# Deformable convolutions on quarters of the matrix array: sums, row spreads and offset convolution in quarter tiles, half-bank sums, row tents' high parts on GpSimd

## What is computed

```python
# x: (4, 64, 24, 24) f32
x = x + _L0_conv_ref(_gn(x), ...)
x = x + _L1_conv_ref(_gn(x), ...)

# one layer, in short
off = conv3x3(x, w_off) + b_off              # 18 offset channels (layer 1: + 9 mask channels)
py = base_y + ky + off_y; px = base_x + kx + off_x
val = corner(y0, x0, wy0 * wx0) + corner(y0, x0 + 1, wy0 * wx1) \
    + corner(y0 + 1, x0, wy1 * wx0) + corner(y0 + 1, x0 + 1, wy1 * wx1)
out = einsum('bckhw,ock->bohw', val * mask, w_def) + b_def
# layer 1 alone: relu(groupnorm over the sample(out))
```

## Time and profile before

| | us |
|---|---|
| median of 3 runs | 170.42 (170.38 to 170.93) |
| the profiled execution | 170.41 |
| its span | 168.6 |
| TensorE busy | 148.6 |
| VectorE busy | 104.9 |
| ScalarE busy | 105.8 |
| GpSimd busy | 68.0 |

### The profile page before, as it was taken

How to read it: one execution, slowest core, us unless ns; L and a number is a source line. 1 busy time by engine, 2 the same in 40 slices (tenths; PEclk the granted TensorE clock), 3 DMA queues, 4 the chain that set the end, 5 groups by cost and what they waited for, 6 DMA issues and landing times.

```text
span 168.6 us, 4694 instructions
## 1 busy us (share of the span) xinstructions
PE 148.6 (88%) x1640; PEld 112.4 (67%) x1640; DVE 104.9 (62%) x248; ACT 105.8 (63%) x243; POOL 68.0 (40%) x131
## 2 busy tenths in 40 slices
PE   7999977999998989997888999998788988979920
PEld 2466634699897766774666876774666867969910
DVE  0526668987675564369986675359975667753133
ACT  3014678889768465379777575379787657864201
POOL 8601355354454434235154434235154425541011
...
GB/s 196 286 251 202 96 34 148 66 2 4 0 6 0 6 2 45 146 60 0 0 4 0 0 8 44 146 61 2 0 6 0 0 10 0 2 70 4 4 6 70
DMA packets 12757, 8.38 MB, mean 50 GB/s; under 512 B 3052, under 2 KB 11820, under 8 KB 12728
## 3 DMA queue, kind: packets, MB, share of 16 engines
...
q10 hardware_dynamic: 288, 0.27, 0.5%
...
## 4 chain that ended last, share of the span: by engine, by line
PE 72%; DVE 12%; issue 9%; ACT 4%; POOL 1%; POOLq 0%; DVEq 0%; ACTq 0%
PE vb L986 18%; PE ob L1006 18%; PE ob L907 11%; PE ring L943 9%; PE ring L951 8%; DVE s L765 5%; PE vb L1081 3%; ACT xa L575 2%; PE ring L895 2%; DVE msk L718 2%; PE ring L926 2%; DVE pos L711 1%; DVE ytent L757 1%; PE ring L885 1%; ACT off L526 1%
## 5 line engine op out<-in xcount | busy, mean ns | idle before, releaser
L487 POOL TENSOR_SCALAR xa<-xa 125x384 f32<-125x384 f32 x108 | 57.5, 538 | 70.1 <-ACT xa L575 69.5
L765 DVE SCALAR_TENSOR_TENSOR s<-xa,ring 125x384 f32<-125x384 f32 x108 | 58.3, 551 | 32.9 <-PE ring L943 28.8
L575 ACT ACTIVATE xa<-ring 125x384 f32<-125x384 f32 x108 | 51.4, 488 | 17.8 <-PE ring L951 17.0
L1006 PE MATMUL ob<-val,w_d 128*64 128x192 f32 x432 | 42.6, 326 | 0.0
L951 PE MATMUL ring<-pos,soon 68*64 68x384 f16 x216 | 37.5, 329 | 3.8 <-DVE s L765 3.1
L943 PE MATMUL ring<-ytent,soon 128*64 128x384 f16 x216 | 37.4, 328 | 3.1 <-DVE ytent L757 1.3
L986 PE MATMUL vb<-s,shifted 125*64 125x216 f32 (+2 forms) x376 | 34.9, 305 | 0.9 <-DVE s L765 0.9
L1006 PEld LDWEIGHTS ob<-val,w_d 128*64 128x64 f32 x432 | 33.7, 136 | 2.5 <-issue 0.4
L986 PEld LDWEIGHTS vb<-s,shifted 125*64 125x64 f32 x376 | 24.5, 136 | 5.0 <-ACT xa L575 1.3
L598 ACT ACTIVATE val<-vb 128x432 f32<-128x432 f32 x33 | 17.5, 530 | 7.4 <-PE vb L986 6.0
L951 PEld LDWEIGHTS ring<-pos,soon 68*64 68x64 f16 x216 | 14.3, 109 | 9.8 <-issue 3.7
...
## 6 DMA issues: line engine op xcount, KB each, us to landing
...
```

The source lines that it names most:

```text
L487: nc.gpsimd.tensor_scalar(v, v, 1.0, 0.0, ALU.min, ALU.max).then_inc(xu_ready, 1)
L575: nc.scalar.activation(xa[:, n % XA_BUFS, :], bank("x", n)[0:SPAN, 0:2 * UPX], ACT.Abs).then_inc(act_took, 1)
L765: nc.vector.scalar_tensor_tensor(out=s[u % 2][:, k // 3:k // 3 + 2 * THIRD, W * k:W * (k + 1)], in0=xa[:, n % XA_BUFS, :].rearrange("q (r ...
L1006: last = mm(sums[64 * i:64 * i + 64, 0:UPX], w_d[l][:, t, 64 * i:64 * i + 64], val[u % 2][:, t // 3:t // 3 + THIRD, W * t:W * (t + 1)], st ...
```

## The change

Seven things change together:

1. The weighted sums use a contraction of 64 lanes (one sample) and 96 pixels, so that a tap is four matmuls on the array's four quarters; their result lies in halves `h` of the unit's rows, `h` = 0 in bank 0 on the samples' own lanes and `h` = 1 in bank 1 on crossed lanes. What reads them does so in three pieces.
2. The offset convolution uses one sample per row half and a quarter of the image per 32 columns: eight matmuls of 144 pixels per tap instead of two of 288. Its result takes two banks of the ring, and ACT reads it in two pieces.
3. The row tents' lanes are rearranged so that a tap's high and low parts lie in one half of the lanes (even taps in lanes 0 to 63, odd taps in 64 to 127). A row spread has a contraction of 64 lanes.
4. Column spreads, row distances and masks have a contraction of at most 60 lanes instead of 68 and 91 (`OFF_LANES`, `MLO`).
5. The high part of the row tents is formed by POOL instead of ACT.
6. The weight blocks lose their zero half; `w_o` is half as large, and two clearing instructions of POOL and a wait of SyncE go.
7. The tables give other orders; a chunk of windows has two parts with due times of their own; the convolutions are one job each; the idle quarters go.

```diff
-OFF_LANES = 68
+OFF_LANES = 60
-MLO = 64
+MLO = 32
-YLO = 64
-YROWS = 2 * YLO
+YLO = 32
+YROWS = 128
+def tent_lane(k, part):
+    return 64 * (k % 2) + YLO * part + ROWS * (k // 2)
 UNIT = {
-    "x": {"PE": -26, "ACT": -26, "POOL": -22}, "s": {"PE": -22, "DVE": -22}, "windows": {"PE": (-1, 2, 4, 6)},
-    "values": {"ACT": (0, 2, 4, 6)}, "weighted": {"PE": (10, 10, 11, 11, 12, 13, 13, 13, 14)},
+    "x": {"PE": -26, "ACT": -26, "POOL": -23}, "s": {"PE": -22, "DVE": -22},
+    "windows": {"PE": (-1, 0, 0, 1, 5, 5, 6, 6)}, "values": {"ACT": (0, 2, 6, 6)},
...
 LAST_UNIT = {
-    "windows": {"PE": (-11, -10, -8, -3, -2)}, "values": {"ACT": (-10, -9, -7, -2, -1)},
-    "weighted": {"PE": (-2, -2, -2, -1, -1, -1, 2, 2, 2)},
+    "windows": {"PE": (-12, -11, -10, -9, -9, -4, -4, -4, -4, -3)}, "values": {"ACT": (-12, -11, -9, 0, 1)},
+    "weighted": {"PE": (1, 2, 2, 2, 3, 3, 6, 6, 6)},
...
-HEAD_PE = [("idle", 11), ("norm", 0), ("idle", 3), ("idle quarters", 3), ("idle", 2), ("xt", (0, 0)), ("xt", (0, 1))] + [("conv", (0, k)) for k in range(5)] \
-    + [("norm", 1)] + [("conv", (0, k)) for k in range(5, TAPS)] + [("conv", (1, k)) for k in range(5)] + [("y", (0, 0))]
+HEAD_PE = [("idle", 11), ("norm", 0), ("idle", 8), ("xt", (0, 0)), ("xt", (0, 1)),
+           ("conv", 0), ("norm", 1), ("y", (0, 0))]
...
+        SUMS = [(0, slice(0, 128), slice(0, 128), 0), (1, slice(64, 128), slice(0, 64), 1), (1, slice(0, 64), slice(64, 128), 1)]
...
-            for l in range(LAYERS):
-                nc.gpsimd.memset(w_d[l][:, :, :], 0.0).then_inc(cleared, 1)
...
+            def y_high(a):
...
+                nc.gpsimd.tensor_scalar(yh[:, :], (yu if m < PAIRS else ym)[:, :], low_y, None, ALU.mult).then_inc(yh_ready, 1)
...
-                nc.scalar.activation(off[:, :], conv_bank(m)[:, 0:HALF], ACT.Identity, bias=b_off[l]).then_inc(t_free, 1)
+                for i in range(2):
+                    wait_full(act, "conv", (m, i))
+                    nc.scalar.activation(off[:, QPX * i:QPX * (i + 1)], bank("conv", (m, i))[:, 0:QPX], ACT.Identity, bias=b_off[l])\
+                        .then_inc(act_took, 1)
...
-                nc.scalar.activation(y[:, p, UPX * j:UPX * (j + 1)], sums[:, 0:UPX], ACT.Identity, bias=b_def[l])\
-                    .then_inc(sums_taken, 1)
+                for b, there, own, h in SUMS:
+                    nc.scalar.activation(y[own, p, half_rows(j, h)], ob[there, b, 0:UPX // 2], ACT.Identity, bias=b_def[l][there, :])\
+                        .then_inc(sums_taken, 1)
...
-                nc.vector.scalar_tensor_tensor(out=x_mid[:, p, c], in0=sums[:, 0:UPX], scalar=b_def[0],
-                                               in1=x_l[:, p, c], op0=ALU.add, op1=ALU.add).then_inc(sums_taken, 1)
+                for b, there, own, h in SUMS:
+                    c = half_rows(j, h)
+                    nc.vector.scalar_tensor_tensor(out=x_mid[own, p, c], in0=ob[there, b, 0:UPX // 2], scalar=b_def[0][there, :],
+                                                   in1=x_l[own, p, c], op0=ALU.add, op1=ALU.add).then_inc(sums_taken, 1)
...
+                for t in range(TAPS):
+                    for i in range(2):
+                        for q in range(QUARTERS):
+                            own = slice(C * i, C * i + C)
+                            last = mm(bank("conv", (m, i))[32 * q:32 * q + 32, 0:QPX], w_o[l][own, t, :],
+                                      pixels(rows_from(m, own, QROWS * q + t // 3, t % 3, QROWS), QROWS),
+                                      start=t == 0, stop=t == TAPS - 1)
...
+                half = slice(64 * (k % 2), 64 * (k % 2) + 64)
                 for d in range(2):
-                    last = mm(bank("s", n)[64 * d:64 * d + 64, 0:2 * UPX], sel[:, k, 64 * d:64 * d + 64],
-                              ytent[u % 2][:, :, :], start=True, stop=True)
+                    last = mm(bank("s", n)[64 * d:64 * d + 64, 0:2 * UPX], sel[half, k, 64 * d:64 * d + 64],
+                              ytent[u % 2][half, :, :], start=True, stop=True)
...
-                for i in range(2):
-                    last = mm(sums[64 * i:64 * i + 64, 0:UPX], w_d[l][:, t, 64 * i:64 * i + 64],
-                              val[u % 2][:, t // 3:t // 3 + THIRD, W * t:W * (t + 1)],
-                              start=t == 0, stop=t == TAPS - 1)
+                for h in range(2):
+                    for i in range(2):
+                        own, to = slice(C * i, C * i + C), C * (i ^ h)
+                        last = mm(ob[to:to + C, h, 0:UPX // 2], w_d[l][own, t, :],
+                                  val[u % 2][own, t // 3 + THIRD // 2 * h:t // 3 + THIRD // 2 * (h + 1), W * t:W * (t + 1)],
+                                  start=t == 0, stop=t == TAPS - 1)
```

249 lines of the change are left out of this document (113 added, 136 removed).

## The result

The changed kernel takes **188.8 us** (median of four, 188.7 to 193.8) against 170.7 for the kernel before (170.4 to 171.6): a ratio of 1.105 with an interval of 1.100 to 1.111. It is 10.5% slower where 9% faster was forecast. The profiled execution is the one of 193.79 us, 2.7% above the other three, which lie within 0.2 us of each other; so the profile shows somewhat more of the low clock than they had.

A forecast was written before the change was run, and what follows sets the result against it. TensorE, 88% busy and 72% of the chain, was taken as the bound until ScalarE and VectorE fill up. 170.4 - 13 (30 to 150 us) - 0.5 (head) - 1.9 (tail) = 155.0 us, range 148 to 162, chance 0.66.

The forecast's parts named there:

- The weighted sums' tap: Weighted sums on TensorE: 0.16 us a tap instead of 0.325, 14.8 us less over ninety taps from 30 to 150 us.
- the convolution: Offset convolution on TensorE: 2.4 us instead of 4.57; two in the 30 to 150 us stretch, 4.3 us less.
- pieces of 96 columns: Reads of the sums: 0.34 us a piece; three replace one, adding 3.0 us for ScalarE and 3.1 for VectorE.
- the share of odd row spreads beside a neighbour: Row spreads, 30 to 150 us: two thirds of 41 odd ones run beside a neighbour, 4.5 us less for TensorE.
- Every rival about the array failing to pack: TensorE: row halves not running side by side, 178 us, chance 0.07; only the sums failing, 171 us, chance 0.05.
- Step 1: GpSimd's twelve high parts: 538 ns each like its clamp, 6.5 us in all, hidden by slack, so costed at nothing.
- Step 2: Stretch 30 to 150 us: TensorE's work falls from 111.8 to 97.0 us; at 91% full it takes 107 us, -13.
- R: Middle stretch: ScalarE and VectorE become the bound through the four-bank ring, 165 us; chance 0.17 (162 to 169).
- the case "slower": Whole kernel slower, chance 0.09; its 178 us came from row halves not running beside each other in real work.
- Step 3: Whole kernel: all prices taken at TensorE's 2.4 GHz, with no term and no rival for a lower clock.
- Step 4: TensorE's list: 103 changes of tile shape, 75 more, at 0.14 us each; 63 in the stretch add 8.8 us.
- Step 5: Head: earlier first convolution, but the second norm and second convolution stand in the way; -0.5 us, between +1 and -1.8.

The follow-up runs named there:

- kernel 8: Kernel before the change, with only the row tents' high parts moved from ScalarE to GpSimd: 188.5 us, ratio 1.106.
- kernel 13: kernel 8 with GpSimd's high part altered (values wrong): first, constant factor or 32-bit output, 188.0 us; second, clamp operations instead of multiplication, 176.9 us.
- kernel 1: Changed kernel with the row tents' high parts moved back from GpSimd to ScalarE: 180.9 us (178.5 to 183.9).
- kernel 12: Kernel before the change, with four of nine taps of every weighted sum left out (results incomplete): 166.4 us, ratio 0.975.
- kernel 7: kernel 6 with the old full-height weighted sums of 192 columns, read in one piece: 179.4 us, ratio 1.040.
- kernel 3: Changed kernel with the old full-height weighted sums of 192 columns, read in one piece: 189.8 us, ratio 1.109.
- kernel 6: kernel 1 with full-height spreads, distances and masks again; sums and convolution stay packed: 175.7 us, ratio 1.026.
- kernel 4: kernel 1 with 21 idle matmuls of zeros in the two waits of the head: 181.4 us (174.8 to 187.7).
- kernel 9: Kernel before the change, with only half-height spreads and lanes added, 188 changes of shape against 28: 184.5 us, ratio 1.083.
- kernel 11: kernel 6 with the second convolution in nine pieces as before the change, written to the sums' banks instead of the ring: 174.1 us (169.8 to 175.4).
- kernel 14: kernel 11 with ten more idle matmuls in the head: 172.7 us; then also two ahead of nine units' windows: 176.2 us.
- A: Theory formed from the profile after: GpSimd's high part is the main cause of the loss; tested by kernel 1, 180.9 us.

## Why the prediction was wrong

Three steps failed where it mattered: GpSimd's high part costed at nothing (18 us alone, 8 in the changed kernel), the stretch of 30 to 150 us taken to shrink nearly as TensorE's list does (-13 us; a microsecond of TensorE is worth a quarter), and every price taken at the full clock (9 to 15 us, an estimate).

**What held.** The weighted sums' tap (0.16 us forecast, 0.17 measured), the convolution (2.4, 2.46), pieces of 96 columns (0.34, 0.34 for ScalarE, with 0.32 for VectorE), a change of shape (0.14, 0.10 to 0.11), the share of odd row spreads beside a neighbour (two thirds, 23 of 36), and which of the two bank rules applies. Every rival about the array failing to pack was wrong.

**Step 1, GpSimd's high part "at nothing".** Two things failed in it. The price: it was costed by the clamp's 0.54 us, and a multiplication takes 1.20 to 1.30 (kernels 8 and 13). Even that step's price without cover, 0.54 us a unit, was for the wrong operation. And the cover: "VectorE has a row spread of slack". The order of the list was read, but not the queue: GpSimd must stand until `yu` or `ym` is there, with clamps for the very next products behind it. The two were measured apart in the kernel before: 11 us for the multiplication (kernel 13's second against the first), 6 us for the rest, which is standing in line and VectorE's sum behind it (0.75 us a unit where it took 0.55). ScalarE, freed of 6 us, gave nothing back that shows. In the changed kernel, whose orders leave more room, taking the high part back gave 8 us (kernel 1), at a clock that stayed low.

**Step 2, "the stretch together", -13 us.** The sum took TensorE's list from 111.8 to 97.0 us and let the stretch follow at 91% full. Kernel 12 shows the rate at which it follows: 4.1 us for 15.6, and between the first and the last unit's sums 2.6 us in the two periods that TensorE fills, 1.0 in the last period and 0.7 in the other eight. Kernels 7 and 3 show it for the packed sums themselves with the changes of shape that go with them: 2 us, and 1 us at another clock. That TensorE is 88% busy and 72% of the chain says it is the last engine at most steps, not that the steps shorten with it. The reading that fits is R: with 1.1 us a tap for 108 taps, and two taps in the ring at a time, each passing through spread, absolute value, clamp and product, a shorter sum mostly becomes a wait for the same bank. Of this the waits are shown and the bank is argued. This was the first rival, at 0.17, and it too was priced too kindly, at 165 us. The case "slower", 178 us, was left behind as well, and its mechanism, an array that does not pack, was not what happened.

**Step 3, not in the sum at all: the clock.** All prices were taken at 2.4 GHz, which the profile of before showed nearly everywhere. In the kernel after the clock is at the lower level in seven stretches. In the 6 us ahead of each, TensorE waited at least once for 0.8 us or more: 3.55 us ahead of the fall at 16.7, 2.09 ahead of that at 71.3. But a wait is not the whole condition: ahead of kernel 1's fall at 126.0 us no wait is longer than 0.3. Kernel 6, with full-height spreads, has no fall in the middle, and kernel 3, with the old sums, has none either. What makes the clock fall stays open.

No run isolates what the low clock costs, but the executions of one kernel, which differ in nothing else on record, give an estimate. The time at the lower level is 2 x (1 - mean clock) x span. The kernel before took 170.4 to 170.6 us with 3 us at that level and 173.7 to 173.9 with 15.5; kernel 4 took 174.8 with 13.5 and 187.7 with 44.5. That is 0.27 to 0.42 us for each. The changed kernel stood there for 38 us, 35 more than the kernel before: 9 to 15 of its 18 us, by this estimate. It also accounts for the 5 us between kernels 1 and 6 (16 us less at the lower level, 4 to 7 us), and it would add some 3 us to what kernel 12 gained (7 of 15.6) and 5 to 7 to what the packed sums bring against kernel 3.

The Trainium skill, TensorE: Matmul & The Clock Gate, section A second HAM failure mode: psum-queue depth-cycling, tells of matmul groups with short idles between them whose clock goes back and forth. This trace agrees that the clock can go back and forth so (seven falls at 79% busy), though no run here shows the short idles to be the cause. The prediction should have carried it as a rival, since the change was made to leave TensorE less to do.

**Step 4, changes of shape.** Their price held; their company did not. Half-height spreads by themselves cost 14 us (kernel 9, 160 changes more) and 5 us in the new orders (1 against 6, 6 changes more and a lower clock), with 4.5 us of gain booked for them in the sum.

**Step 5, the head, -0.5 us.** It was +7.4. The ring was named there as what the second convolution blocks, and priced inside +1 to -1.8. Measured: 1.7 us remain once that convolution leaves the ring (kernel 11), 0.8 once the clock stays up too (kernel 14). The rest was GpSimd's 1.25 us in the chain to the first row tents, the low clock, and the ring.

**The sum as measured,** with the steps in one order: 188.8 to 180.9 us by A, to 175.7 by full-height spreads, to 174.1 by the head, against 170.5. The last 3.6 us go with the clock: 169.8 and 171.9 where it stayed up. One thing was not tested: the share of the chain in which nothing shown was waited for (issue) is 9% of 168.6 us before, 11% of 191.9 after and 14% of 173.3 in kernel 6, that is 15, 21 and 24 us, while TensorE's instructions went from 1640 to 2483. A part of what packing gave may have gone there.
